# Causal attention stage: row scores and five other products take turns in two pairs of banks

## The reference

```python
q_lat = (x @ Wq_down).reshape(b, t, H, L)          # k_lat, v_lat alike
q_c, q_e = q_lat @ Wq_up_c, q_lat @ Wq_up_e        # per head; k and v alike
q = concat([q_c, rope(q_e)]); k = concat([k_c, rope(k_e)])
scores = einsum('bhqd,bhkd->bhqk', q, k) / sqrt(8)
scores = where(causal, scores, -inf)
att = softmax(scores)
y = einsum('bhqk,bhkd->bhqd', att, v)
return y.transpose(0, 2, 1, 3).reshape(b, t, c) @ Wc
```

## Time and profile before

| | before |
|---|---|
| median of 3 runs | 4020.49 us (4016.85 to 4025.2) |
| profiled execution | 4023.4 us |
| its span | 4021.5 us |
| PE busy | 3620.6 us, 90% of the span |
| DVE busy | 3032.2 us, 75% |
| ACT busy | 2850.0 us, 71% |
| POOL busy | 2423.1 us, 60% |

### The profile page before, as it was taken

The page is one execution under the profiler, slowest core; times in us unless marked ns, Lnnn a source line. Parts: engine busy times, 40 slices in busy tenths (PEclk is TensorE's granted clock), DMA queues, the critical chain, the costliest instruction groups (busy, mean ns, idle before and its releaser), DMA issues.

```text
span 4021.5 us, 98070 instructions
## 1 busy us (share of the span) xinstructions
PE 3620.6 (90%) x31846; PEld 2751.9 (68%) x32224; DVE 3032.2 (75%) x4780; ACT 2850.0 (71%) x6080; POOL 2423.1 (60%) x2185
## 2 busy tenths in 40 slices
PE   5888868999989999979999889999899999799998
PEld 3444436777667777657777567776677776577776
DVE  4665538888678888678887688886688886788876
ACT  2444447888668888668887578886588886688875
POOL 1111117777457777467776477775577774677763
PEclk9998979999989999989999999999899999899999
DMA  3222210000100000100000100001000001000002
GB/s 123 71 66 77 61 45 2 0 0 0 28 2 1 0 0 0 28 2 1 0 0 1 29 2 0 0 0 28 2 2 0 0 0 29 2 1 0 0 1 70
DMA packets 59737, 67.80 MB, mean 17 GB/s; under 512 B 12006, under 2 KB 40164, under 8 KB 58468
## 3 DMA queue, kind: packets, MB, share of 16 engines
q1 hardware_dynamic: 59492, 64.64, 5.6%
HBM read 46.27 MB, written 18.35 MB: 16 GB/s over the span
## 4 chain that ended last, share of the span: by engine, by line
PE 30%; issue 23%; ACT 21%; DVE 21%; ACTq 1%; DVEq 1%; POOL 1%; DMA 0%; SPq 0%; POOLq 0%
PE bank L387 26%; ACT sb_area L772 10%; DVE sb_ssq L1280 9%; DVE sb_smax L1291 5%; ACT sb_area L911 5%; DVE sb_area L1132 3%; ACT sb_lnb L923 2%; ACT sb_lnb L920 2%; PE bank L607 2%; PE bank L636 1%; POOL sb_area L1505 1%; DVE sb_area L1268 1%; DVE sb_area L1294 0%; PE bank L665 0%; ACT sb_wqk_hi L772 0%
## 5 line engine op out<-in xcount | busy, mean ns | idle before, releaser
L772 ACT ACTIVATE sb_area<-bank 128x512 f32<-128x512 f32 (+3 forms) x2533 | 1359.0, 577 | 268.7 <-PE bank L387 205.7
L1268 DVE TENSOR_TENSOR sb_area<-bank,sb_rots 128x1024 f32<-128x1024 f32 x768 | 939.4, 1225 | 398.4 <-ACT sb_area L911 397.3
L387 PE MATMUL bank<-sb_area 128*64 128x64 f32 (+5 forms) x17616 | 1113.7, 273 | 71.8 <-issue 57.6
L1480 POOL TENSOR_TENSOR sb_area<-sb_area,sb_rn 128x512 f32<-128x512 f32 x768 | 784.8, 1043 | 609.5 <-ACT sb_rn L927 609.5
L1466 POOL TENSOR_TENSOR sb_area<-sb_area 128x512 f32<-128x512 f32 x768 | 967.8, 1278 | 91.6 <-DVE sb_area L1268 87.9
L387 PEld LDWEIGHTS bank<-sb_area 128*64 128x64 f32 (+4 forms) x17616 | 767.3, 144 | 186.6 <-issue 133.0
L387 PE MATMUL bank<-sb_wqk_hi,sb_xwin 128*128 128x512 f32 x1536 | 725.6, 474 | 58.5 <-DVE sb_xwin L1248 48.1
L387 PE MATMUL bank<-sb_area,sb_wvo 128*128 128x256 f32 x3072 | 728.5, 381 | 3.1 <-DVE sb_xT L1326 3.1
L387 PEld LDWEIGHTS bank<-sb_area,sb_wvo 128*128 128x128 f32 x3072 | 556.3, 191 | 77.2 <-issue 12.8
L607 PE MATMUL bank<-sb_ident,sb_area 128*128 128x128 f32 x3072 | 491.9, 284 | 38.3 <-ACT sb_area L772 32.5
L607 PEld LDWEIGHTS bank<-sb_ident,sb_area 128*128 128x128 f32 x3072 | 356.5, 143 | 230.9 <-issue 160.2
(11 more groups left out here) (113 smaller groups left out, 4153.2 us busy)
## 6 DMA issues: line engine op xcount, KB each, us to landing
qk_rows<-sb_p SPq DMA_DIRECT2D x52, 256.0 KB, 4.0
sb_wqk_hi<-qk_rows SPq DMA_DIRECT2D x32, 256.0 KB, 2.9
sb_wqk_lo<-qk_rows SPq DMA_DIRECT2D x32, 256.0 KB, 2.7
sb_area<-in_Wqkv SPq DMA_DIRECT2D x7, 1024.0 KB, 5.9
sb_area<-in_WvT SPq DMA_DIRECT2D x7, 512.0 KB, 7.6
sb_wo_bd<-in_Wo SPq DMA_DIRECT2D x14, 256.0 KB, 8.6
sb_area<-in_x SPq DMA_DIRECT2D x4, 512.0 KB, 6.3
sb_area<-in_x SPq DMA_DIRECT2D x8, 256.0 KB, 3.1
```

What stands on the lines that cost most here:

```text
L387: return nc.tensor.matmul(o, a, b, start=start, stop=stop, skip_group_check=True)
L772: return nc.scalar.activation(o, i, ACT.Copy)
L1268: tt_(t12[:, c % 2, :, :].rearrange("p u (h d) -> p u h d", h=8), src, bc(rots[:, tt, s, :, :], [P, 2, 8, D], 2), ALU.mult).then_inc(S["ro ...
L1480: pt_(qn[:, c, :].rearrange("p (h d) -> p h d", h=8), qsum[:, c % 2, :].rearrange("p (h d) -> p h d", h=8), r, ALU.mult).then_inc(S["qn"], 1)
```

## The change

Nothing that is computed changes. What is done:

- Banks 0 to 3 become two pairs. Row units, the turned maxima, values, output, rotation and sums take turns in them, in the one order `order`; a turn waits until the turn two before it has been read (`free_banks`), by DVE (`rows_read`) or by ACT (`rows_read_act`).
- Both rotation products of a side (`i` = 0, 1) go into one turn. DVE's stages move: the queries' stages 0 to 3 to k = 1 and 4 to k = 2, the keys' 0 to 2 to k = 2, 3 and 4 to k = 3.
- Column pairs use three banks, 4 to 6, in turn, and wait for one exponential more. Weighing has bank 7.
- `et0`, `et1`, `et2` are double, by n % 2. Weighing is one piece, for slot s - 3, behind unit 0 and ahead of `turn_max`; before, two pieces were at the start of a step and one each in the middle and near the end.
- In PE's order the units stand closer: 1 and 2, 3 and 4 around a pair. On ACT the inversion of the sums stands ahead of pair 4's exponentials rather than behind.

```diff
-        et0, et1, et2 = take(4, T), take(4, T - P), take(4, T - P)
+        et0, et1, et2 = take(2, 4, T), take(2, 4, T - P), take(2, 4, T - P)
...
+                if there:
+                    reader = "rows_read_act" if op[0] in by_act else "rows_read"
+                    turn[op] = len(order)
+                    order.append((reader, count[reader] + 1))
+                    count[reader] += 1
+                    ordinal[op] = count[reader]
+
+        def rows_banks(*op):
+            first = 2 * (turn[op] % 2)
+            return banks[:, first:first + 2, :]
...
-            def bank_m(*op):
-                need(pe, "m_free", m_at[op])
-                return ps[7]
-
-            def project_causal(a, i):
-                mm(bank_m("rope", a, i), wcomb[:, i, :], xT[:, a * T:(a + 1) * T]).then_inc(S["c_proj"], 1)
+            def free_banks(*op):
+                if turn[op] >= 2:
+                    reader, reads = order[turn[op] - 2]
+                    pe.wait_ge(S[reader], reads)
+                return rows_banks(*op)
+
+            def project_causal(a, side):
+                o = free_banks("rope", a, side)
+                for i in range(2):
+                    mm(o[:, i, :], wcomb[:, 2 * side + i, :], xT[:, a * T:(a + 1) * T]).then_inc(S["c_proj"], 1)
...
             def rows_of_scores(n, u):
                 hg, x, qt = n % 4, u // 4, u % 4
-                need(pe, "c_max", 8 * n + u)
+                o = free_banks("unit", n, u)
...
             def columns_of_scores(n, p):
                 hg, T_, x = n % 4, p // 2, p % 2
-                need(pe, "c_exp", 12 * n + 2 * p - 2)
+                need(pe, "c_exp", 12 * n + 2 * p - 1)
...
-                b0 = ps[2 + 2 * p % 4], ps[3 + 2 * p % 4]
+                o = ps[4 + 2 * p % 3], ps[4 + (2 * p + 1) % 3]
...
-            def weigh_causal(n, kt):
+            def weigh_causal(n):
                 a, hg = n // 4, n % 4
-                pe.wait_ge(S["c_exp"], 12 * n + (4, 8, 12, 12)[kt])
...
+                pe.wait_ge(S["c_exp"], 12 * n + 12)
...
                 pair(0)
+                unit(0)
+                if slot(n2 - 1):
+                    weigh_causal(n2 - 1)
                 if slot(n1 - 1):
                     turn_max(n1 - 1)
-                unit(0)
-                weigh(n2 - 1, 2)
-                weigh(n2 - 1, 3)
                 pair(1)
                 unit(1)
+                unit(2)
+                pair(2)
...
-                pair(2)
-                unit(2)
-                weigh(n2, 0)
                 unit(3)
                 pair(3)
+                unit(4)
...
-                unit(4)
+                unit(5)
                 pair(4)
-                unit(5)
-                weigh(n2, 1)
+                unit(6)
                 pair(5)
-                unit(6)
                 unit(7)
...
-                need(act, "c_pv", 12 * (n - 1) + 4 * T_ + 4)
+                need(act, "c_pv", 4 * (n - 1))
...
                 exp_pair(n2, 3)
-                exp_pair(n2, 4)
                 if half_done:
                     sums_inverted(a, j)
+                exp_pair(n2, 4)
                 exp_pair(n2, 5)
```

More of the change, by code:

```diff
@@ L265, in slot @@
             return 0 <= n < SLOTS
-        m_at = {}
+        by_act = ("v", "perm")
+        turn, ordinal, count = {}, {}, {"rows_read": 0, "rows_read_act": 0}
+        order = []
         for s in range(FIRST, LAST + 1):
[L269 to L274, removed]
-                if there:
-                    m_at[name] = len(m_at)
+            k = s % 4
+            for op, there in ((("unit", s, 0), slot(s)), (("max", s - 1), slot(s - 1)), (("unit", s, 1), slot(s)),
+                              (("unit", s, 2), slot(s)),
+                              (("v", s // 4), k == 0 and valid(s // 4)), (("out", (s - 9) // 4), k == 1 and valid((s - 9) // 4)),
+                              (("rope", (s + 6) // 4, 1), k == 2 and valid((s + 6) // 4)),
+                              (("unit", s, 3), slot(s)), (("unit", s, 4), slot(s)),
+                              (("perm", (s - 4) // 4, 0), k == 0 and valid((s - 4) // 4)),
+                              (("rope", (s + 7) // 4, 0), k == 1 and valid((s + 7) // 4)),
+                              (("perm", (s - 6) // 4, 1), k == 2 and valid((s - 6) // 4)),
+                              (("unit", s, 5), slot(s)), (("unit", s, 6), slot(s)), (("unit", s, 7), slot(s))):
+                if there:
+                    reader = "rows_read_act" if op[0] in by_act else "rows_read"
[6 more added lines that the diff above has]
+            return banks[:, first:first + 2, :]
         def need(eng, name, v):
@@ L342, in _ @@
                     a = (s - 9) // 4
-                    sp.wait_ge(S["m_free"], m_at["out", a] + 1)
+                    sp.wait_ge(S["rows_read"], ordinal["out", a])
                     sp.dma_start(scr[a], xres[:, 1, :, :]).then_inc(S["ca_out"], 16)
@@ L486, in weigh_causal @@
                     need(pe, "c_yraw", 2 * a + hg // 2)
-                e, c0 = ((et0, 0), (et1, 0), (et2, 0), (et2, 2 * P))[kt]
-                for r in range(4):
-                    m = mm(ps[6][32 * r:32 * r + 32, kt * P:T], v32[:, a % 2, (kt * 4 + r) * 2 + hg // 2, hg % 2, :],
-                           e[:, r, c0:c0 + T - kt * P], hg % 2 == 0 and kt == 0, hg % 2 == 1 and kt == 3)
-                    if kt != 2:
-                        m.then_inc(S["c_pv"], 1)
+                for kt in range(TT):
+                    e, c0 = ((et0, 0), (et1, 0), (et2, 0), (et2, 2 * P))[kt]
+                    for r in range(4):
+                        m = mm(ps[7][32 * r:32 * r + 32, kt * P:T], v32[:, a % 2, (kt * 4 + r) * 2 + hg // 2, hg % 2, :],
+                               e[:, n % 2, r, c0:c0 + T - kt * P], hg % 2 == 0 and kt == 0, hg % 2 == 1 and kt == 3)
+                        if kt == 3:
+                            m.then_inc(S["c_pv"], 1)
```

137 lines of the change are left out of this document (63 added, 74 removed).

## The result

The changed kernel takes 3955.47 us (3950.38 to 3958.9), the kernel before 4018.67 us in the same set of runs; the ratio is 0.984, with a 95% interval of 0.982 to 0.986. Forecast were 3954 us and a range of 3890 to 4000. The profiled execution of after has a span of 3956.9 us against 4021.5, so 64.6 us less.

A forecast was written before the change was run, and what follows sets the result against it. It took the bound to be PE and DVE alternating on one pair of banks, neither engine's throughput. From 4023.4 us, -47 - 10 - 13 + 3 = -67 gave 3956, or 3954 as median; range 3890 to 4000.

The forecast's parts named there:

- The bound: Causal stage: row units and their reductions alternate strictly on one pair of banks, 12.1 of 14.1 us a slot.
- The 30 slots: Causal stage, 30 slots between turnings of the maxima: 1.58 us less a slot, 47 us in all, clock apart.
- the walk: One slot of each kind stepped through its waits: k = 3 10.1, k = 0 12.4, k = 1 14.0, k = 2 13.7 us.
- The clock: Causal stage: of 24 us lost to the lower clock level in 30 slots, 10 are regained.
- The start: Slots 0 and 1, from first unit to the turning: 33.9 us become 20.5, gain taken as 13.
- The end: Last slots of the causal stage: they end with the whole weighing instead of its second half, +3 us.
- (4): One-piece weighing, 2.47 us, ahead of the turning: delays the turning and what follows; DVE idles 1.5 to 2 us.
- (3): Column pairs on three banks instead of four: pairs can't be closer than some 1.25 us, waiting for ACT's exponentials.
- A: Rival, causal stage: PE becomes the bound at 10.4 us a slot; 3874, halfway there 3915; chance 0.2.
- B: Rival: SP's loop from turning to next keys binds, 11.3 to 13.2 us; 3994 us; chance 0.2.
- C: Rival: ring turns and three banks give back the gain; slot stays at 14.1, 4020 us; chance 0.04.
- D: Rival: slower because much of PE's work runs at the lower clock; 4050 us at 40%; chance 0.06.

The follow-up runs named there:

- e1_late_division: The changed kernel with DVE's division in slots with k = 1 moved behind the maximum of unit 2; 3942.8 us, 0.981 of the kernel before.
- e2_turn_first: The changed kernel with the turning of the maxima put ahead of the weighing on PE; 3986.0 us, 0.991 of the kernel before.
- e11_half_output: e1_late_division with half of the causal output product left out (four of eight matmuls per batch); 3945.1 us, 0.981 of the kernel before.

## Why the prediction was right

The time, the direction and the sum were right; the terms one by one:

- **The bound.** Strict alternation of a unit and its reduction. DVE's wait for units fell from 182.7 to 56.5 us, and one pair of banks gives 4225 us where two give 3943, or 4048 by the estimate above with the clock's part taken off. That the new arrangement lives by the second pair is shown; what the rows' pair gives alone was not run.
- **The 30 slots.** Forecast -47 and -10 for the clock, measured -54.5 in all, but the agreement is of the sum only. Four full slots at full clock went from 56.5 to 52.7 us, not to the 50.2 of the walk. With 8, 8, 7 and 7 slots of each kind (k = 2, 3, 0, 1) that is 423.8 against 393.3 us, so -30.5 where the walk said -47: the largest term was too large by half.
- **Where the walk was off.** k = 0 was walked at 12.4 and is 12.42, k = 2 at 13.7 and is 13.3. k = 3 was walked at 10.1 and is 11.2. I put that down to the rotation's stages and the division on DVE, since slots at full clock that have only one of the two take 10.5 (the first, no division) and 10.4 to 10.6 (the last two, no rotation); no run tested it. k = 1 was walked at 14.0 and is 15.8 at full clock. The step that failed there is the one on that slot, "output and the two query rotations": I read DVE's order as "division, output, rotation" and priced them, but didn't ask what the division waits for. The wait on `ca_mm` was in the order's own rows. Moving it gives back 12.7 us.
- **What made up for it.** The walk gave every slot all its products. The first and last batches lack some, and a slot without them shrinks more: the last goes from 13.2 to 10.4 us. The 30 slots of after measure 393.3 us, just what 30 full slots at full clock would, though the lower level costs them some 12 us (next point). So the short slots save about 12, which the forecast did not have. -30.5, -12 for the clock, -12 for the short slots, -12.8 for the start, +6.4 for the end and -3.7 in the six layers make the 64.6 us. That 3954 comes so close to 3955 is luck.
- **The clock.** 0.93 became 0.95, and I took 10 of 24 us. In after seven of 30 slots have a clock under 1.00. Five are longer than the same kinds at full clock by 1.1 to 2.2 us, and two in the last batches have no equal; by the slots of e1_late_division they lose some 1 and 3.6. An estimate of what is still lost is 12 us: the term was about right. Of the start the prediction says "at the lower level"; the trace of before prints a clock of 1.00 up to some 100 us, but the durations bear the prediction out, 2.07 us for one rotation product there against 0.99.
- **The start.** -13, measured -12.8: the first unit comes 2.0 us earlier (60.11 us against 62.09), and from it to the turning at 83.22 are 23.1 us, where 33.9 had been and 20.5 were walked.
- **The end.** +3, measured +6.4. The last weighing stands alone behind an idle PE and runs at the lower level (granted clock 0.50), 4.5 us in place of 2.4, which is two of the 3.4 us missed:

```profile
496.79 4.50 PE L401 MATMUL bank<-sb_area 128*32 128x512 f32 x32 [1.01 <-ACT sb_area L834]
```

- **Parts.** (4) was the best of them: DVE idle in front of the rests, foreseen as 1.5 to 2 us, is 2.31 in the slot shown and 2.06 on average. What I understated is its price. By itself it costs 63 us in the old order, the clock's part included, and 16 to 23 in the new one can be had back by cutting it up. (3) costs nothing alone and up to 24 us of PE's waits in the new order; what those waits cost the slot was not isolated.
- **Rivals.** A, PE alone at 10.4 us a slot, did not come: the best version has slots of 12.2, 14.6, 13.0 and 10.1. B, the loop through SP: in the slot from 279.14 us on the next keys are issued at 282.64, 11.3 us ahead of unit 0 of the next slot, and PE nowhere stands behind a DMA in the stage's list of waits. C, no gain, with the rule of the Trainium skill ("TensorE: Matmul & The Clock Gate", section "HAM oscillation — how this bites in real kernels") that in one matmul kernel double-buffered PSUM gave no further gain: the runs of this case disagree, 282 us between one pair and two, of which, by the estimate above, at least 105 are not the clock. The 1.03 us in front of the turning, which the prediction gives there as a wait for a bank, is no such wait: the turning needs the last unit's maxima themselves. The wait for a bank is the 1.08 us ahead of a row unit. D, the clock, did not come in after, but it is real: in e2_turn_first the stage's clock fell to 0.88 and the kernel was 30 us slower, of which up to 24 can be the clock, and in e11_half_output less work was no faster.

## What to carry to other kernels

When two engines alternate on one buffer, add up the latencies between them: here the units with their reductions were 12.1 of 14.1 us. A second buffer took DVE's wait for units from 182.7 to 56.5 us, but a full slot only from 14.1 to 13.2, because other waits stepped in. Once the buffer is shared by a ring of different products, every wait in a reader's queue ahead of its turn becomes PE's wait, so go through each reader's order and ask of each instruction what it waits for, not only what it costs. And long work of the producer belongs in pieces where the consumer has something queued, not in one piece in front of what the consumer needs next. When an edit costs or gains more than the walk says, look at the clock of the slots before blaming the wait: compare slots of the same kind at full clock, and then the totals.

## What the runs showed of the hardware

The granted clock of PE moved with small edits that changed no work: over the stage 0.93 before, 0.95 after, 0.97 with the division moved, 0.98 with the weighing in two pieces, 1.00 with three, 0.88 with turning and weighing swapped, 0.91 with the sums read late, 0.85 with the weighing in one piece in the old kernel, and 0.67 with one pair of banks; 0.95 with a part of the work left out. So a later read could cost more than its own length: with the sums read late it is 1.05 us in a slot at full clock, but 31 us in all over 14 such slots. The pair of rotation products takes 1.98 us at the full level (2.4 GHz) and 3.5 where the granted clock is 0.54, nearly all at the lower one (1.2 GHz), and in after it fell there in slots in which PE had idled 1.75 us at one gap and 0.75 at another shortly before; but at 335.65 us a slot with the same gaps kept the full clock. What decides between the two was not found.
